# A graph layer's prologue: edge lists and tables first, the node features beside them, and the first normalization in groups

## What is computed

```python
def _layernorm(x, axis=-1, eps=1e-05):
    m = jnp.mean(x, axis=axis, keepdims=True)
    v = jnp.var(x, axis=axis, keepdims=True)
    return (x - m) / jnp.sqrt(v + eps)
...
    edge_index = jnp.stack([src, dst])
    x = x + _L0_gnn_ref(_layernorm(x, axis=-1), edge_index, L0_gnn_W, L0_gnn_b)
    x = x + _L0_ffn_ref(_layernorm(x, axis=-1)[None], L0_ffn_Wg, ...)[0]
    x = x + _L1_gnn_ref(_layernorm(x, axis=-1), edge_index, L1_gnn_W, ...)
    x = x + _L1_ffn_ref(_layernorm(x, axis=-1)[None], L1_ffn_sW1, ...)[0]
```

## Time and profile before

| what | value |
|---|---|
| median of 3 runs | 3672.1 us (3669.44 to 3673.27) |
| the profiled execution's own time | 3671.94 us |
| its span in the profile | 3670.2 us |
| mean granted clock of PE | 0.875 |
| busy: PE, DVE, ACT, POOL | 76%, 50%, 26%, 47% of the span |

### The profile page before, as it was taken

The page is one execution under the profiler, slowest core; times in us unless marked ns, Lnnn a source line. Parts: engine busy times, 40 slices in busy tenths (PEclk is TensorE's granted clock), DMA queues, the critical chain, the costliest instruction groups (busy, mean ns, idle before and its releaser), DMA issues. The chain is left out here.

```text
span 3670.2 us, 56109 instructions
## 1 busy us (share of the span) xinstructions
PE 2801.8 (76%) x13194; PEld 2306.5 (63%) x13195; DVE 1850.6 (50%) x4258; ACT 965.1 (26%) x3415; POOL 1719.0 (47%) x1811
## 2 busy tenths in 40 slices
PE   1477888887874999999995647766776776738999
PEld 0356666666663888888884535555555555538998
DVE  5324454444556111111113758778887778773444
ACT  0001110000010222222221334333443333325554
POOL 0677777777770222232221177766666667200000
PEclk9888888888887999999997868888888888857999
DMA  5333333333330222222222543333333333100000
GB/s 170 94 105 110 110 116 110 110 109 110 109 108 15 81 81 86 83 86 83 85 84 84 171 110 106 104 103 101 100 102 103 102 102 104 43 17 9 20 21 20
DMA packets 152206, 327.38 MB, mean 89 GB/s; under 512 B 38743, under 2 KB 89905, under 8 KB 147938
## 3 DMA queue, kind: packets, MB, share of 16 engines
q0 software_dynamic: 85824, 236.38, 22.8%
q1 hardware_dynamic: 59762, 83.04, 6.8%
q10 hardware_dynamic: 6480, 6.42, 0.5%
HBM read 286.42 MB, written 41.40 MB: 89 GB/s over the span
## 5 line engine op out<-in xcount | busy, mean ns | idle before, releaser
L633 POOL DMA_INDIRECT G<-g_rows,srcT x784 | 743.1, 948 | 426.3 <-issue 237.2
L633 POOL DMA_INDIRECT G<-h_rows,srcT x784 | 752.3, 960 | 251.8 <-issue 237.0
L1728 PE MATMUL pS<-G,O 128*128 x2336 | 639.2, 437 | 56.9 <-DVE O L1876 55.8
L817 PE MATMUL pS<-G,O 128*128 x2336 | 569.7, 408 | 142.2 <-SPq L804 108.6
L817 PEld LDWEIGHTS pS<-G,O 128*128 128x128 f32 x2336 | 476.4, 206 | 231.9 <-issue 153.3
L1728 PEld LDWEIGHTS pS<-G,O 128*128 128x128 f32 x2336 | 492.6, 214 | 199.4 <-issue 83.3
L1361 PE MATMUL pH<-XT,w1s 128*128 128x256 f32 x1728 | 384.0, 381 | 0.9 <-DVE XT L1401 0.9
L1371 PE MATMUL pY<-w2s,HE 128*128 128x256 f32 x1728 | 381.9, 379 | 0.0
L1361 PEld LDWEIGHTS pH<-XT,w1s 128*128 128x128 f32 x1728 | 329.8, 191 | 46.5 <-issue 1.3
L1386 ACT ACTIVATE HE<-pH,b1s 128x256 f32<-128x256 f32 x432 | 204.9, 474 | 583.2 <-PE pH L1361 583.2
L1293 POOL DMA_INDIRECT y_rows<-YE,yidx x108 | 109.3, 1012 | 527.3 <-DVE YE L1413 510.8
(11 more groups left out here) (301 smaller groups left out, 3535.2 us busy)
## 6 DMA issues: line engine op xcount, KB each, us to landing
w1s<-in_W_dram SPq DMA_DIRECT2D x16, 1024.0 KB, 5.2
w2s<-in_W_dram SPq DMA_DIRECT2D x16, 1024.0 KB, 8.0
G<-h_rows,srcT POOLq DMA_INDIRECT x784, 2.7
Y<-y_rows SPq DMA_DIRECT2D x49, 256.0 KB, 4.4
G<-g_rows,srcT POOLq DMA_INDIRECT x784, 2.8
g_rows<-OUT SPq DMA_DIRECT2D x49, 132.0 KB, 2.5
h_rows<-ACC SPq DMA_DIRECT2D x7, 896.0 KB, 5.4
X<-in_x_dram SPq DMA_DIRECT2D x1, 6144.0 KB
```

The source lines that it names most:

```text
L633: pool.indirect_dma_start(out=G[:, c % (ring * Q), 0:width], out_offset=None, in_=rows, in_offset=bass.IndirectOffsetOnAxis(ap=srcT[:, c:c ...
L817: mm = nc.tensor.matmul(pS[k][:, 0:W], O[:, k, q, :], G[:, bass.ds((s % R0) * Q + q, 1), :].rearrange("p a d -> p (a d)"), start=(q == 0), ...
L1728: mm = nc.tensor.matmul(pS[:, bass.ds((w % BANKS) * BANK, NR)], O[:, k, q, :], G[:, bass.ds((s % R) * Q + q, 1), 0:NR].rearrange("p a d -> ...
```

## The change

The blocks keep their order. What moves:

- `X` is loaded from ACT's queue, in seven pieces of seven tiles (and the last tile), each with a semaphore of its own, `s_x[c]`. SP's queue has only the lists.
- Block one's DVE goes straight to the lists. Statistics, normalization and the stores of `h0_rows` leave block one.
- They come back in block two, behind the tables in DVE's list. For each of seven groups of seven tiles DVE takes the statistics, the small moments (`ln_group`, as the later stages do), the reciprocal of the group before and its `shift` (minus mean times reciprocal). ACT takes the root of the group and applies scale and shift with 49 `Identity` activations in place of DVE's 49 `tensor_scalar`. SP stores each group when it is ready and waits for all stores before the block ends.
- In block three the memset of `G`'s column of ones and the signal `s_ready` stand ahead of the memset of `ACC`.
- 14 unused semaphores go, seven come (`s_x`).

```diff
                         for lst, name in ((src_sorted, "src"), (dst_sorted, "dst")):
                             sp.dma_start(lst[0:z.E].rearrange("(a b) -> a b", a=16),
                                          a[name].rearrange("(a b) -> a b", a=16)).then_inc(s_lists, 16)
-                        sp.dma_start(X[:, 0:FULL, :], a["x"][0:FULL * P, :].rearrange("(t p) d -> p t d", p=P))\
-                            .then_inc(s_x, 16)
-                        sp.wait_ge(s_const, 1)
-                        sp.dma_start(X[0:REST, FULL, :], a["x"][FULL * P:N, :]).then_inc(s_x, 16)
                         sp.wait_ge(s_pads, 2)
...
-                        for t in range(0, NT, UNROLL):
-                            sp.wait_ge(s_h0, t + UNROLL)
-                            sp.dma_start(h0_rows[t * P:(t + UNROLL) * P, :].rearrange("(t p) d -> p t d", p=P),
-                                         ACC[:, t:t + UNROLL, 0:D]).then_inc(s_h0st, 16)
                         store_gaps(sp, s_rowsf, s_gaps)
-                        sp.wait_ge(s_h0st, 16 * (NT // UNROLL))
...
                     @block.scalar
                     def _(act):
-                        ln_root(act, s_var, s_root)
+                        assert NT % UNROLL == 0 and FULL == NT - 1
+                        for c in range(XCH):
+                            t0, t1 = c * UNROLL, min((c + 1) * UNROLL, FULL)
+                            act.dma_start(X[:, t0:t1, :], a["x"][t0 * P:t1 * P, :].rearrange("(t p) d -> p t d", p=P))\
+                                .then_inc(s_x[c], 16)
+                        act.wait_ge(s_const, 1)
+                        act.dma_start(X[0:REST, FULL, :], a["x"][FULL * P:N, :]).then_inc(s_x[XCH - 1], 16)
...
-                        dve.wait_ge(s_x, 32)
-                        all_stats(dve, s_stat)
-                        dve.wait_ge(s_stat, NT)
-                        ln_moments(loc, s_var)
-                        ln_rstd(loc, s_root)
-                        each_tile(dve, lambda t, k: ln_apply(ACC[:, bass.ds(t, 1), 0:D], X[:, bass.ds(t, 1), :],
-                                                             bass.ds(t, 1)).then_inc(s_h0, 1), UNROLL)
                         rows_ready(loc, s_rows, s_rowsf)
...
+        def apply_h0(act, c):
+            act.wait_ge(s_norm, c + 1)
+            for t in range(c * UNROLL, (c + 1) * UNROLL):
+                nc.scalar.activation(ACC[:, t, 0:D], X[:, t, :], ACT.Identity, bias=shift[:, t:t + 1],
+                                     scale=rstd[:, t:t + 1]).then_inc(s_h0, 1)
...
+                @block.sync
+                def _(sp):
+                    for c in range(XCH):
+                        t0, t1 = c * UNROLL, (c + 1) * UNROLL
+                        sp.wait_ge(s_h0, t1)
+                        sp.dma_start(h0_rows[t0 * P:t1 * P, :].rearrange("(t p) d -> p t d", p=P), ACC[:, t0:t1, 0:D])\
+                            .then_inc(s_h0st, 16)
+                    sp.wait_ge(s_h0st, 16 * XCH)
+
+                @block.scalar
+                def _(act):
+                    for c in range(XCH):
+                        act.wait_ge(s_var, c + 1)
+                        ln_group_root(c * UNROLL, (c + 1) * UNROLL).then_inc(s_root, 1)
+                        if c:
+                            apply_h0(act, c - 1)
+                    apply_h0(act, XCH - 1)
+
...
+                    def normal(c):
+                        v = slice(c * UNROLL, (c + 1) * UNROLL)
+                        dve.wait_ge(s_root, c + 1)
+                        ln_group_rstd(loc, v.start, v.stop)
+                        loc.link(nc.vector.scalar_tensor_tensor(out=shift[:, v], in0=mean[:, v], scalar=-1.0,
+                                                                in1=rstd[:, v], op0=ALU.mult, op1=ALU.mult))
+                        dve.sem_inc(s_norm, 1)
+
+                    for c in range(XCH):
+                        dve.wait_ge(s_x[c], 32 if c == XCH - 1 else 16)
+                        for t in range(c * UNROLL, (c + 1) * UNROLL):
+                            nc.vector.bn_stats(stats[:, t, :], X[:, t, :]).then_inc(s_stat, 1)
+                        dve.wait_ge(s_stat, (c + 1) * UNROLL)
+                        ln_group(loc, c * UNROLL, (c + 1) * UNROLL)
+                        dve.sem_inc(s_var, 1)
+                        if c:
+                            normal(c - 1)
+                    normal(XCH - 1)
...
                     loc = Local(dve, s_dve)
+                    loc.link(nc.vector.memset(G[:, :, D:D + 1], 1.0))
+                    dve.sem_inc(s_ready, 1)
                     loc.tick(nc.vector.memset(ACC[:], 0.0))
                     loc.tick(nc.vector.tensor_copy(iota_p, iota_n[:]))
-                    loc.tick(nc.vector.memset(base[:, 0], 0.0))
-                    loc.link(nc.vector.memset(G[:, :, D:D + 1], 1.0))
-                    dve.sem_inc(s_ready, 1)
+                    loc.link(nc.vector.memset(base[:, 0], 0.0))
```

More of the change, by code:

```diff
@@ L142, in build @@
         s_gath_l1 = [sem(f"s_gath_l1_{k}") for k in range(R)]
-        s_sent = [sem(f"s_sent{k}") for k in range(7)]
-        s_got = [sem(f"s_got{k}") for k in range(7)]
+        XCH = NT // UNROLL
+        s_x = [sem(f"s_x{k}") for k in range(XCH)]
         s_sort = [sem(f"s_sort{k}") for k in range(4)]
@@ L190, in ln_rstd, with ln_group, ln_group_root, ln_group_rstd @@
             loc.link(nc.vector.reciprocal(rstd[:], lnt[:, 2]))
+        def ln_group(loc, t0, t1):
+            m, s = stats[:, t0:t1, :], lnt[:, :, t0:t1]
+            loc.tick(nc.vector.tensor_tensor(s[:, 0], m[:, :, 1], m[:, :, 4], ALU.add))
+            loc.tick(nc.vector.tensor_tensor(s[:, 1], m[:, :, 1], m[:, :, 4], ALU.subtract))
+            loc.link(nc.vector.tensor_tensor(s[:, 2], m[:, :, 2], m[:, :, 5], ALU.add))
+            loc.tick(nc.vector.tensor_scalar(mean[:, t0:t1], s[:, 0], 0.5, None, ALU.mult))
+            loc.link(nc.vector.scalar_tensor_tensor(out=s[:, 1], in0=s[:, 1], scalar=0.25, in1=s[:, 1],
+                                                    op0=ALU.mult, op1=ALU.mult))
+            loc.link(nc.vector.scalar_tensor_tensor(out=s[:, 1], in0=s[:, 2], scalar=1.0 / D, in1=s[:, 1],
+                                                    op0=ALU.mult, op1=ALU.add))
+            loc.link(nc.vector.tensor_scalar(s[:, 0], s[:, 1], LN_EPS, None, ALU.add))
+        def ln_group_root(t0, t1):
+            return nc.scalar.activation(lnt[:, 2, t0:t1], lnt[:, 0, t0:t1], ACT.Sqrt)
+        def ln_group_rstd(loc, t0, t1):
+            loc.link(nc.vector.reciprocal(rstd[:, t0:t1], lnt[:, 2, t0:t1]))
         def ln_apply(out_ap, in_ap, t):
@@ L268, in build @@
                 pV = ps("pV", [P, 512])
-                s_x = sem("s_x")
                 s_pads = sem("s_pads")
@@ L278, in build @@
                 s_viol = sem("s_viol")
[L279 to L283, removed]
                 s_dve = sem("s_dve")
@@ L301, in _ @@
                         load_lists(sp, s_rows)
-                        assert NT % UNROLL == 0
-                        for t in range(0, NT, UNROLL):
-                            sp.wait_ge(s_h0, t + UNROLL)
-                            sp.dma_start(h0_rows[t * P:(t + UNROLL) * P, :].rearrange("(t p) d -> p t d", p=P),
-                                         ACC[:, t:t + UNROLL, 0:D]).then_inc(s_h0st, 16)
                         store_gaps(sp, s_rowsf, s_gaps)
-                        sp.wait_ge(s_h0st, 16 * (NT // UNROLL))
                     @block.gpsimd
@@ L551, in build @@
             s_tabs = sem("s_tabs")
+            s_stat = sem("s_stat1c")
+            s_var = sem("s_var1c")
+            s_root = sem("s_root1c")
+            s_norm = sem("s_norm1c")
+            s_h0 = sem("s_h01c")
+            s_h0st = sem("s_h0st1c")
             s_dve = sem("s_dve1c")
+            shift = sb("shift", [P, NT])
             with nc.Block() as block:
+                @block.sync
[14 more added lines that the diff above has]
+                    apply_h0(act, XCH - 1)
                 @block.gpsimd
@@ L661, in tiles_of @@
             return range(FIRST[g], FIRST[g + 1]) if 0 <= g < NG else range(0)
[L663 to L680, removed]
         ADST = make(top)[0]("ADST", [P, NT, HEADS])
```

## The result

The kernel after takes 3659.94 us (median of 12 runs, 3655.74 to 3668.18) against 3671.74 for the kernel before in the same series (12 runs): 11.8 us less, ratio 0.9968 with an interval of 0.9960 to 0.9975. The forecast was 3655.7 us, 16.4 less. The profiled execution took 3661.2 us with a span of 3659.5.

What follows compares the result with a forecast made beforehand. POOL's steady gather pace from its first gather was taken to set the stage's end. Block three 3.4 us earlier plus 13.0 inside it made 16.4 off 3671.94, with the median 0.2 above: 3655.7 us, range 3646 to 3667.

Steps and rivals of the forecast that it cites:

- The path: Prologue to end of gather stage: POOL's steady pace sets the end, one microsecond off the first gather is one off the end.
- First gather inside block three: In block three: with the signal ahead of DVE's long memset, the first gather comes 13.0 us earlier.
- The other reading, 11.1: DVE's memset in block three begins where its row does, so the first gather moves only 11.1 us.
- Start of block three: Prologue up to block three: it starts at 87.2 us in place of 90.6, 3.4 us earlier.
- I take 21, nearest to equal shares: Prologue: lists land at 21 us, sharing the transfer engines about equally with the features; bounds 14.3 and 25.
- The 8.3 for the issue: SP's queue in the prologue: padding issues at some 3.6 us plus 4.7 to land, 8.3 us before the row loads.
- ACT's 0.40 us: Normalization in block two: ACT's 49 activations of 256 columns come 0.40 us apart, 14 of them after DVE's groups.
- The memset holds POOL up: Block three: DVE's long memset stops POOL's gathers, 13.0 us of gain are gone, 3668.7 us; chance 7%.
- PE can't use the head start: Gather stage: PE's later waits don't shrink, the stage gains only PE's 6.9 us, 3661.8 us in all; chance 5%.
- Table loads on ACT: Normalization: each switch between root and `Identity` loads a table, 14 x 1.28 us, gain only 2.9, 3669.2 us; chance 3%.
- The clock in the last stage: Last stage: PE's clock rises later by X us of work, costing X/2; 3680.7 us at X = 50; chance 5%.
- The lists don't get through: Prologue: engines serve features first, lists land at 34 us as before, gain only 3.4, 3668.7 us; chance 10%.

Runs made afterwards that it cites:

- e1: Kernel before, with only the memset of G's column and the signal moved ahead of the memset of ACC: 3659.61 us, ratio 0.9968.
- e2: Kernel after, with only the signal and memset order undone, so the signal comes last again: 3672.02 us, ratio 1.0001 to the kernel before.
- e3: Kernel after, but ACT's queue issues two of seven feature pieces at once, the others when the lists' rows have landed: 3648.25 us, ratio 0.9933.
- e6: e3 with each group's reciprocal and shift after the next group's second statistics, ACT applying it right behind its root: 3644.92 us, ratio 0.9924.
- e7: e6 with the first group's seven statistics ahead of DVE's wait for PE's table products: 3648.09 us, ratio 0.9934.
- e12: e7 with all features issued behind the lists' rows, no piece first: 3643.93 us, ratio 0.9927 to the kernel before.
- e10: e3 with four of the seven feature pieces issued at once instead of two: 3658.08 us, one run.
- e11: e3 with no feature piece issued before the lists' rows have landed: 3647.56 us, one run.
- e9: Kernel after, with the memset of ACC split in two, 25 and 24 tiles: 3661.97 us, one run.

## Why the prediction was right, and where not

**The path** (POOL's pace from its first gather): right. The first gather moved by -9.3, -13.7, +3.6, -20.5, -21.5, -23.9 and -27.6 us in after, e1, e2, e3, e6, e7 and e12, and the medians by -11.8, -11.5, +0.9, -22.9, -26.6, -23.4 and -24.3. Within 5 us that is one for one, and but for e6 (22.8 to 32.7 us less by its interval) the first gather's step lies within each interval. The traces show it closer. The end of the stage (ACT's table load behind it) moved by -7.8, -14.3, +3.6, -14.4, -21.0, -23.9 and -27.6. e3 is the exception, and e10 and e11, with -10.7 and -18.1 against -15.2 and -22.5 at the first gather, go with it. In these three the last gather is in time within 1.5 us, but from there to the stage's end it is 84.0 to 85.4 us in place of 80.5 to 82.2, and PE's mean granted clock over that stretch is 0.69 in place of 0.75 to 0.78 (PE is busy 56.7 us there in e3 and 50.5 before).

**First gather inside block three, 13.0 us**: right to the tenth, and the reading of the memset's row with it. The other reading, 11.1, is excluded: in the trace after DVE has done the small memset at 94.45 and the row of the large one still begins 2.9 us later, and e9 splits that gap. e1 has this term without the rest of the change: 1.29 us from the block's start to the first gather.

**Start of block three, 3.4 us earlier**: wrong in sign; it was 3.7 later. By terms, forecast and then measured: lists' rows 21.0 and 26.8 (+5.8); casts, columns and tables 27.1 and 27.4 (+0.3); DVE's seven groups with the last shift 28.3 and 28.8 (+0.5, a group is 4.13, not 4.0); from there to ACT's end 5.0 and 6.5 (+1.5); store and block's end 5.8 and 4.8 (-1.0). The sum is 7.1. The time came out only 4.6 us above the forecast: the first gather alone accounts for 9.3 of the 11.8 us (the interval is 9.2 to 14.7), the other 2.5 are not explained, and to that extent the forecast's nearness is luck. What the change gains comes from the 13.0 us alone.

The largest miss is "I take 21, nearest to equal shares". Shared engines were the right mechanism, its size was not, and the rows came later than the 25 of the bounds too. The 8.3 for the issue was 9.2. Then the prediction has 12 us, twice the 6.0 of the loads alone, and the kernel after has 4.1 us without a packet and 12.8 us with packets one for one against the features' larger ones; 0.7 us later DVE's cast begins. The delay ahead of the first packet had no term in the sum. e3, e10 and e11 show that the features' traffic is the cause. It is not the rival at 34 us either, in which the features go first: they don't, from 13.3 us on.

The second miss is ACT's 0.40 us, from activations that had at most a bias per partition; these have bias and scale, and start 0.49 apart. The Trainium skill has this price (ScalarE: Activation LUTs, What ACT_TABLE_LOAD costs), 93 ns for each operand per partition; the rows of 585 and 492 ns agree. The prediction didn't draw on it.

**The rivals.** *The memset holds POOL up*: excluded: nine gathers of 0.95 us with 0.30 between them ran beside it, as the others do. *PE can't use the head start*: excluded by e1, though PE's first item moved by less than I worked out: in the kernel after it is 22.7 us into the block against 26.6 before, 3.8 sooner and not 6.9. The bias pieces end 19.8 us into the block, near the 19.6 worked out, but PE starts 2.9 us after that; before, the wait for the gathers covered it. *Table loads on ACT*: excluded, one load in the prologue. *The clock in the last stage*: the rise came earlier with the stage. *The lists don't get through*: not so, but they came 5.8 us late, as said above.

**Open**: whether e2's 3.6 us are in its time; its interval holds both. Also open are the 2.5 us by which the kernel after gained more than its first gather, and why PE's granted clock was lower at the stage's end in e3, e10 and e11. Why the rows' first packet waits 4.1 us was not tried.

## What to carry to other kernels

When one engine's steady work sets a stage, look at what stands ahead of its first instruction before rebuilding what lies further up: a signal that waited behind an unrelated memset was worth as much as the whole change. A small load does not get half of the engines beside a bulk one because it has a queue of its own: look at the packets of both. A transfer on a second queue still shares the engines, so one that isn't needed yet should be issued behind the one that is; and where a diff does several things, undo them one at a time: here two parts had opposite signs.

## What the runs showed of the hardware that I had not expected

- The row of a long DVE memset begins late: 10.84 us shown of 13.7 (e9: 5.56 and 5.34 shown, with 1.55 and 1.27 of "issue" ahead). The idle time of DVE directly ahead of these memsets is largely the memset.
- Two queues with loads in flight shared the transfer engines packet for packet, not byte for byte: 863 packets each from 21 to 25 us, 0.43 MB in rows of 512 bytes against 0.87 MB in rows of 1 KB; over the 18 us from 9 to 27 they moved 334 GB/s together.
- The first packet of a small load came 4.1 us after its issue with four or seven pieces of 0.9 MB issued on the other queue, and 1.0 to 1.2 us after it with none or two. By both effects each piece cost the lists 1.0 to 2.7 us (first cast at 13.51, 15.54, 20.93 and 26.79 with 0, 2, 4 and 7 pieces).
- Seven stores issued 4.0 us apart in the mean landed 4.0 to 4.2 us after issue; issued 2.3 us apart they took 4.1 to 6.9.
